# A DRAM operand laid out by groups of two head pairs, fetched by one group ahead of the first block

## The reference

```python
def _phi(x, omega):                       # omega: 16 x 128
    proj = jnp.einsum('bhtd,dm->bhtm', x, omega)
    norm_sq_half = 0.5 * jnp.sum(x * x, axis=-1, keepdims=True)
    return jnp.exp(proj - norm_sq_half) / math.sqrt(m)
phi_q, phi_k = _phi(q, omega), _phi(k, omega)
S = jnp.cumsum(phi_k[..., :, None] * v[..., None, :], axis=2)
Z = jnp.cumsum(phi_k, axis=2)
y = einsum(phi_q, S) / (einsum(phi_q, Z) + EPS)
h = _layernorm(x) * (1 + ca) + sa
x = x + ga * attn(h)
h = _layernorm(x) * (1 + cb) + sb
x = x + gb * ffn(h)
```

## Time and profile before

| | us |
|---|---|
| median of 3 runs | 792.42 (791.97 to 794.87) |
| the profiled execution | 791.14 |
| its span, first to last instruction | 788.9 |
| PE busy | 740.5 (94% of the span) |
| DVE busy | 526.3 (67%) |
| ACT busy | 422.1 (53%) |

### The profile page before, as it was taken

How to read it: one execution, slowest core, us unless ns; L and a number is a source line. 1 busy time by engine, 2 the same in 40 slices (tenths; PEclk the granted TensorE clock), 3 DMA queues, 4 the chain that set the end, 5 groups by cost and what they waited for, 6 DMA issues and landing times.

```text
span 788.9 us, 17005 instructions
## 1 busy us (share of the span) xinstructions
PE 740.5 (94%) x6138; PEld 605.5 (77%) x6138; DVE 526.3 (67%) x1265; ACT 422.1 (53%) x769; POOL 62.7 (8%) x72
## 2 busy tenths in 40 slices
PE   3889999999999999999999999999999999999696
PEld 3678768887698867887688876987678876987466
DVE  4366776676666776766776767767766767766456
ACT  3376636664556554665366745575456644564232
POOL 1260010001000010001000010000100010000100
PEclk9999999999999999999999999999999999999799
DMA  8750183103801065102811057010741029000000
GB/s 282 198 143 2 54 211 64 53 0 118 205 2 53 27 188 111 53 0 80 208 38 53 0 146 179 9 44 27 212 87 53 0 89 223 13 29 28 0 1 27
DMA packets 42804, 65.36 MB, mean 83 GB/s; under 512 B 5000, under 2 KB 19104, under 8 KB 42656
## 3 DMA queue, kind: packets, MB, share of 16 engines
q1 hardware_dynamic: 42784, 65.09, 30.6%
HBM read 39.91 MB, written 25.17 MB: 82 GB/s over the span
## 4 chain that ended last, share of the span: by engine, by line
PE 79%; DVE 12%; issue 3%; DMA 2%; ACT 2%; POOL 1%; DVEq 0%; SPq 0%; ACTq 0%; POOLq 0%
PE pa L579 11%; PE prod L592 7%; PE ring L428 6%; PE ring L558 5%; PE pa L428 5%; PE pa L430 5%; PE pa L429 5%; PE ring L430 4%; PE ring L429 4%; PE ring L612 4%; PE ring L563 3%; PE ring L720 2%; PE ring L619 2%; PE pa L693 2%; DVE am_phk L1178 2%
## 5 line engine op out<-in xcount | busy, mean ns | idle before, releaser
L579 PE MATMUL pa<-phq,phkT 128*128 128x128 f32 x768 | 101.2, 275 | 0.0
L1178 DVE TENSOR_TENSOR am_phk<-pa,const 128x512 f32<-128x512 f32 x112 | 77.0, 688 | 35.6 <-PE pa L579 34.6
L579 PEld LDWEIGHTS pa<-phq,phkT 128*128 128x128 f32 x768 | 95.4, 192 | 2.1
L1348 DVE SCALAR_TENSOR_TENSOR am_phk<-ring,am_phk 128x512 f32<-128x512 f32 x64 | 44.3, 691 | 53.2 <-PE ring L773 53.2
L988 ACT ACTIVATE qk_r<-phq 128x512 fp32r<-128x512 f32 x64 | 40.5, 633 | 63.7 <-DVE phq L1357 63.7
L428 PE MATMUL pa<-wo_r,qk_r 128*128 128x256 f32 x256 | 72.2, 282 | 0.6 <-DVE qk_l L1353 0.6
L430 PE MATMUL pa<-wo_l,qk_r 128*128 128x256 f32 x256 | 72.3, 282 | 0.0
L429 PE MATMUL pa<-wo_r,qk_l 128*128 128x256 f32 x256 | 72.0, 281 | 0.0
L558 PE MATMUL ring<-xq,omega_x 100*128 100x512 f32 x196 | 70.3, 440 | 1.4 <-DVE lora_w L1171 1.4
L918 ACT ACTIVATE phq<-ring 128x512 f32<-128x512 f32 x82 | 49.3, 602 | 36.1 <-PE ring L558 34.9
L918 ACT ACTIVATE phkT<-ring 128x512 f32<-128x512 f32 x98 | 58.3, 595 | 12.9 <-PE ring L558 12.6
(11 more groups left out here) (209 smaller groups left out, 1609.3 us busy)
## 6 DMA issues: line engine op xcount, KB each, us to landing
xq<-qk_parts SPq DMA_DIRECT2D x48, 512.0 KB
qk_parts<-qk_r SPq DMA_DIRECT2D x32, 256.0 KB, 4.4
qk_parts<-qk_l SPq DMA_DIRECT2D x32, 256.0 KB, 4.9
tok<-in_L_attn_x SPq DMA_DIRECT2D x8, 512.0 KB, 3.6
xr<-in_L_attn_x SPq DMA_DIRECT2D x8, 512.0 KB, 3.4
out_x<-tg SPq DMA_DIRECT2D x16, 256.0 KB, 2.2
norm_parts<-norm_r SPq DMA_DIRECT2D x16, 128.0 KB, 2.3
norm_parts<-norm_l SPq DMA_DIRECT2D x16, 128.0 KB, 2.4
```

What stands on the lines that cost most here:

```text
L579: mm = pe.matmul(score_bank(q, a)[:, tt], phkT[:, q % 2, a, tt], query(q)[:, a, tt], start=True, stop=True)
L1178: dve.tensor_tensor(am[:, 2 * (q % 2) + a, :].rearrange("p (c t) -> p c t", c=NT), score_bank(q, a)[:].rearrange("p (c t) -> p c t", c=NT) ...
L1348: dve.scalar_tensor_tensor(r2[:, f % 2, :], z_bank[f % 4][:], 0.0, rho, ALU.max, ALU.mult).then_inc(r2_done.sem, 1)
```

## The change

- `qk_parts` becomes (part, half, group of two pairs, q or k, 64 channels, tokens), so that the fetch of one group is one access. A send, whose source is still 128 partitions, now writes two pieces of 64 rows: the written side of the transfer is 2 x 64 x 512 instead of 128 x 512.
- `norm_parts` holds only the rows that are used. A half's norms are sent by four transfers of 8 rows instead of two of 64 rows, and fetched by one transfer with four rows on the written side instead of two transfers with two.
- `xq` gets a dimension for the group. In the loop the fetch of q and k has the same size and order as before.
- In set-up SP first fetches group 0 of half 0 alone, counted in a semaphore of its own (`lead_moved`), then sends the second half, then fetches group 1 (`moved[0]`) and the second half. PE's tile 0 in the lead waits for `lead_moved`; before tile 12, at the start of `attend`, PE waits for `moved[0]`.

```diff
-        xq = sb("xq", [XROWS, 2, 2, HALF, T], F32R)
+        xq = sb("xq", [XROWS, 2, 2, 2, HALF // 2, T], F32R)
...
-        norm_out = [sig(name, 2 * 16) for name in ("norm0_out", "norm1_out")]
-        moved = [sig(name, 5 * 16) for name in ("moved0", "moved1")]
+        norm_out = [sig(name, 4 * 16) for name in ("norm0_out", "norm1_out")]
+        moved = [sig(name, 4 * 16) for name in ("moved0", "moved1")]
+        lead_moved = sig("lead_moved")
...
+            def send(n, j):
+                wait(sp, qk_split, n, j + 1)
+                for part, src in enumerate((qk_r, qk_l)):
+                    sp.dma_start(parts_out[part, j // 2, :, j % 2], src[:, j, :].bitcast(F32)).then_inc(qk_out[j // 2].sem, 16)
+
+            def send_norms(n, half):
+                for part, src in enumerate((norm_r, norm_l)):
+                    for kind in range(2):
+                        row = (2 * half + kind) * VA
+                        sp.dma_start(norms_out[half, part, :, :, kind].rearrange("a g i t -> (a g) i t"),
+                                     src[row:row + 2 * GROUP, :].bitcast(F32)).then_inc(norm_out[half].sem, 16)
+
+            def fetch_qk(n, half, quarter, signal):
+                wait(sp, qk_out[half], n, qk_out[half].per)
+                for copy, part in enumerate((0, 0, 1)):
+                    src = parts_out[part, half, quarter].rearrange("g k (i r) t -> r (g k i) t", r=PAIR_ROWS)
+                    sp.dma_start(xq[copy * PAIR_ROWS:(copy + 1) * PAIR_ROWS, half, quarter]
+                                 .rearrange("r g k i t -> r (g k i) t").bitcast(F32), src).then_inc(signal.sem, 16)
+
+            def fetch_norms(n, half, quarter, signal):
+                wait(sp, norm_out[half], n, norm_out[half].per)
+                src = norms_out[half, :, :, quarter].rearrange("q a g k i t -> (q a) (g k i t)")
+                sp.dma_start(xq[3 * PAIR_ROWS:XROWS, half, quarter].rearrange("r g k i t -> r (g k i t)").bitcast(F32),
+                             src).then_inc(signal.sem, 16)
+            def first_front():
+                send(0, 0)
+                send(0, 1)
+                wait(sp, norm_split, 0, 1)
+                send_norms(0, 0)
+                fetch_qk(0, 0, first, lead_moved)
+                fetch_norms(0, 0, first, lead_moved)
+                send(0, 2)
+                send(0, 3)
+                wait(sp, norm_split, 0, 2)
+                send_norms(0, 1)
+                fetch_qk(0, 0, second, moved[0])
+                fetch_norms(0, 0, second, moved[0])
+                fetch_qk(0, 1, both, moved[1])
+                fetch_norms(0, 1, both, moved[1])
...
-                    if tile == 0:
+                    if tile == 0 and lead:
+                        pe.wait_ge(lead_moved.sem, 4 * 16)
+                    if tile == 0 and not lead:
                         wait(pe, moved[0], n, moved[0].per)
...
                 pe.wait_ge(late_vec.sem, 10)
+                pe.wait_ge(moved[0].sem, moved[0].per)
                 features(n, 2, first)
...
-    parts_out = nc.dram_tensor("qk_parts", (2, 4, P, T), F32, kind="Internal").ap()
-    norms_out = nc.dram_tensor("norm_parts", (2, P, T), F32, kind="Internal").ap()
+    parts_out = nc.dram_tensor("qk_parts", (2, 2, 2, 2, P // 2, T), F32, kind="Internal").ap()
+    norms_out = nc.dram_tensor("norm_parts", (2, 2, 2, 2, 2, 2, T), F32, kind="Internal").ap()
```

More of the change, by code:

```diff
@@ L330, in _ @@
             sp.sem_inc(scaled.sem, scaled.per)
[L332 to L356, removed]
@@ L358, in next_front @@
-            def next_front(n):
[L360 to L390, removed]
-                wait(sp, norm_split, n, 2)
[L392 to L396, removed]
@@ new lines, in _ @@
+            first, second, both = slice(0, 1), slice(1, 2), slice(0, 2)
+            def first_front():
[13 more added lines that the diff above has]
+                fetch_norms(0, 1, both, moved[1])
@@ L398, in load_xr @@
+            def next_front(n):
+                send(n, 0)
+                send(n, 1)
+                fetch_qk(n, 0, both, moved[0])
+                send(n, 2)
+                send(n, 3)
+                wait(sp, norm_split, n, 2)
+                send_norms(n, 0)
+                send_norms(n, 1)
+                fetch_norms(n, 0, both, moved[0])
+                fetch_qk(n, 1, both, moved[1])
+                fetch_norms(n, 1, both, moved[1])
             def load_xr(n):
@@ L407, in ffn_stores @@
                                  tg[:, b, :].rearrange("p (t c) -> p t c", t=2)).then_inc(out_done.sem, 16)
-            front_moves(0)
+            first_front()
             sp.wait_ge(wp_done.sem, B)
@@ L557, in features @@
                     if k < 4:
-                        mm = pe.matmul(dst[:], omega_x[:, k // 2 * M:(k // 2 + 1) * M], xq[:, p // HALF, k % 2, p % HALF, :],
+                        mm = pe.matmul(dst[:], omega_x[:, k // 2 * M:(k // 2 + 1) * M], xq[:, p // HALF, p // 2 % 2, k % 2, p % 2, :],
                                        start=True, stop=True)
@@ L562, in features @@
                             t = (2 * (k - 4) + c) * P
-                            mm = pe.matmul(dst[:, c * 2 * M:(c + 1) * 2 * M], xq[:, p // HALF, 1, p % HALF, t:t + P], omega_x[:],
+                            mm = pe.matmul(dst[:, c * 2 * M:(c + 1) * 2 * M], xq[:, p // HALF, p // 2 % 2, 1, p % 2, t:t + P], omega_x[:],
                                            start=True, stop=True)
```

## The result

The changed kernel takes **1066.24 us** (median of 4 runs, 1065.12 to 1067.18) against 792.19 us (4 runs, 791.18 to 794.87): 1.3446 times the time before, 95% interval 1.3415 to 1.3478. The profiled execution took 1067.06 us with a span of 1064.8 us; its mean granted clock is 0.859 against 0.991 (1.00 is the upper of TensorE's two levels, 2.4 GHz, and 0.50 the lower, 1.2 GHz).

A forecast was written before the change was run, and what follows sets the result against it. PE was taken as the bound, with the DRAM round trip hidden but for 4 us. 791.1 plus 26.6 for set-up, 241.5 for the loop and 8 for the clock gave 1067 us, range 1005 to 1120.

The forecast's parts named there:

- Two engines for a send: Sends of q and k: writing 2 x 64 x 512 runs on two DMA engines, 5.65 us of data against 0.7 before.
- Rate, 23.2 GB/s for each engine, and 1.3 us around the data: Each send: a busy engine moves 23.2 GB/s, with 1.3 us more around the data; four sends of a half take 22.6 us.
- The path in the loop: Each of seven blocks: slow sends delay the fetch, norm sends, DVE's masks and PE's tile 0, 34.5 us per block, 241.5 in all.
- Set-up: Before the loop: tile 0 13.0 us later, tile 12 waits for group 1 until 80.8 (lower bound 79); +26.6 us in all.
- The clock, 8 us, at most 12.8: PE after eight new stalls: granted clock falls, 1.0 us taken for each, 8 in all, between 0 and 12.8.
- The signs in the profile: Profile after: DMA share near 0.13, PE waits about 17 and 13 us, DVE 34 in seven blocks, passes of 126 to 127.
- SP held back: SP's queue before its fetch: queue limits holding SP back there were named as something that could make the sum alone wrong.
- The rival with sixteen engines: Sends keep sixteen engines because the read side decides: 785.5 to 792 us, near 787; 12 in 100.
- Its price for norm sends: In the loop under the sixteen-engine case: eight norm issues delay the masks 0 to 0.7 us per block, 5 in all.
- The rule that it gave: Norm sends under the sixteen-engine case: the kernel gets faster while an issue costs under 0.5 us.
- Slower engines: Rival for the sends: two engines at 13 GB/s each, a send 10 us, a half 40, near 1350 us; 3 in 100.
- No overlooked cover: Rival at the masks: narrow sends are hidden anyway by an overlooked cover, which would have to hold 34 us; 1 in 100.

The follow-up runs named there:

- the first experiment: The changed kernel with each q and k send issued as two transfers writing 64 x 512, not one writing 2 x 64 x 512: 808.64 us, 1.0205 times before.

## Why the prediction was right

The forecast was 1067 us and slower; 1066.24 was measured. The mechanism and the path were right; that the total came within 1 us is luck, since two errors of nearly 9 us cancel in it. By its steps:

- **Two engines for a send.** Right: share 0.13 while sends run alone, and the sends split in two bring back 258 of 274 us. The rule of the Trainium skill (DMA: Bandwidth & Descriptors, "Why a DMA increments its semaphore by 16 and not by 1") holds here for mixed sides, 128 partitions read and 2 or 4 pieces written: 0.13 and 0.26 of sixteen engines.
- **Rate, 23.2 GB/s for each engine, and 1.3 us around the data.** Both off, in opposite directions: 51 / 2 = 25.5 and 2.8. A half that nothing else delays took 23.4 us, against 23.9.
- **The path in the loop.** Right in order and size. For the first pass, on the clock of before (27.09 taken off), the fetch of half 0 is issued at 118.7 (119.2 predicted), DVE runs at 149.9 (151.9), tile 0 at 153.3 (153.9). The second half's sends start behind the fetch, without a start of their own, and gain the 2 us of the better rate; the norm fetch then took 4.2 us instead of 2.6 and gave 1.6 back. Tile 0 moved by 33.5 per pass in the mean (34.5), seven passes 234.8 (241.5).
- **Set-up.** Tile 0 at 54.2 (53.9), tile 12 at 78.7 (80.8; the lower bound 79 was nearer), tile 24 at 90.5 without a wait (90.0). To tile 12 that is +24.5 (26.6).
- **The clock, 8 us, at most 12.8.** This is the term that was mis-sized. 275.9 - 24.5 - 234.8 leaves 16.6, above the bound: 27.1 - 24.5 = 2.6 in set-up and 14.0 in the passes. I had taken 1.6 us, what the 4 us stall of before cost, as the most that one stall can cost. Behind tile 12 PE ran 6.0 us at 0.50, which misses 3.0 us of full clock, and behind a pass's stall there were some nine (the windows above), the first 2.6 of them ahead of tile 0.
- **The sum** hit because the waits were 8.8 us too long in it and the clock 8.6 too short; the 1 us on the total says less than the terms do. The spreads that the prediction names add up to less than its range of 1005 to 1120, which was set wider than they give.
- **The signs in the profile** came: shares of 0.13, waits of 17.5 and 12.6 us at the lead and 33 at the masks in seven blocks, passes of 126.5 to 127.3 us.
- **SP held back** was named as something that could spoil the sum. It happened (issues of up to 7.9 us), and the traces show no cost of it: while SP was held in the second half's sends, the two engines stayed at 0.13 and 52 GB/s without a gap, and what SP had next to do waited for the same sends, or stood behind them. No run takes the holding away alone.
- **The rival with sixteen engines** has no run of its own, since single sends of 2 x 64 x 512 did not run so; the kernels with 64 x 512 and 128 x 512 sends come nearest. Its lead came true, in part in the first experiment (first loop send 4.1 us earlier) and wholly with whole sends (5.6, of 4.0 to 5.6 predicted). Its price for norm sends did not: 0 to 0.7 us per pass was 2.7. The rule that it gave, faster only while an issue costs under 0.5 us, was right: at 0.60 the kernel is 2% slower; with issues of 0.30 the one with split sends is 0.4% faster and the one with whole sends 0.9%. What it left out is what follows once the cover of DVE's L1340 is gone: DVE's 0.6 more of waiting, PE's wait for `xq` (8.7 us in eight, of which 1.8 at the lead) and a stretch of half clock in four of the seven passes, in which PE's busy time grows from 740.5 to 747.8.
- **Slower engines** (1350) was wrong: 25.5 GB/s each. **No overlooked cover** was there.

## What to carry to other kernels

Look at both sides of every transfer for the outermost dimension: a DRAM layout that splits the rows into two separate pieces (2 x 64 x 512 for 128 x 512) put a wide store on two engines here, with the same bytes and rows. If a part is to be fetched earlier, cut it on the reading side, and leave the write one run of rows; here that gave 0.9% where the layout lost 34%. On a queue whose issues stand in line for a reader with less than 2 us to spare, the time of an issue is a cost like that of a transfer, and a small stall on PE can cost its clock as well.

## What the runs showed that I had not expected

- An issue can block its engine: with two engines for a transfer, the third and fourth send of a half kept SP 1.4 to 7.9 us each, 3.8 and more in most cases, and so did the norm send behind them (up to 5.0). With four engines single issues took up to 5.3. 128 x 512 on sixteen engines took 0.33 and 0.44 in the median.
- What a DMA costs SP depends on its shape, not its bytes: 8 x 512 read and written 0.30 us, the same bytes written as 4 x 2 x 512 0.58 to 0.63 in the median, 64 x 512 0.60, 128 x 512 0.33 to 0.44. What in the shape decides isn't settled: 64 x 512 has the same shape on both sides.
- The low clock outlasts a stall by unlike times: half clock ended about 3.2 us after PE's restart at 54.16, after 6.0 us of work at tile 12, and more than 9 us after PE's restart behind the 33 us stall of a pass. The cost behind tile 0 was yet 1.6 to 2.5 us per pass. In the first pass, from tile 0 at 180.39 to the end at about 187, half clock misses some 3.4 us by its share, and 2.2 show; that PE also waits for other engines there may hide the rest, and was not tried.
- Equal stalls need not bring the clock down: behind 1.15 and 0.85 us it fell in some passes of the first experiment's kernel and not in others.
